# Splitting attention's small solves into halves between large matmuls, and preparing their operands earlier on VectorE

## The reference, cut to what matters

```python
x = x + 0.5 * moe(layernorm(x))
x = x + attn(layernorm(x))
x = x + 0.5 * moe(layernorm(x))
...
# attention, per sequence and head (4 heads of 32), in 8 chunks of 32 tokens
attn = -einsum('bhncd,bhned->bhnce', kbc, kc) * strict_lower
for i in range(1, chunk):
    upd = einsum('...j,...ji->...i', attn[..., i, :], attn[..., :, :i])
    attn = attn.at[..., i, :i].add(upd)
attn = attn + eye(chunk)
u = attn @ vc          # the values solve
w = attn @ kbc         # the keys solve
# then a scan over the 8 chunks
ui = ui - wi @ S; oi = qi @ S + a_loc @ ui; S = S + ki^T ui
...
# a multiscale causal convolution of v over 31 lags, a small gating network,
# a softmax mixture of the three branches, an RMS norm and an output projection
```

## Time and profile before

| | us |
|---|---|
| median of 3 runs | 1126.39 |
| lowest and highest run | 1124.57 and 1128.73 |
| the profiled execution | 1120.73 |
| its span, first to last instruction | 1118.9 |
| TensorE busy | 854.6 (76% of the span) |
| VectorE, ScalarE, GpSimd busy | 543.9, 335.9, 465.5 |
| mean granted TensorE clock | 0.898 |

### The profile page before, as it was taken

How to read it: one execution, slowest core, us unless ns; L and a number is a source line. 1 busy time by engine, 2 the same in 40 slices (tenths; PEclk the granted TensorE clock), 3 DMA queues, 4 the chain that set the end, 5 groups by cost and what they waited for, 6 DMA issues and landing times. The chain is left out here.

```text
span 1118.9 us, 26929 instructions
## 1 busy us (share of the span) xinstructions
PE 854.6 (76%) x11563; PEld 751.8 (67%) x11563; DVE 543.9 (49%) x1569; ACT 335.9 (30%) x646; POOL 465.5 (42%) x588
## 2 busy tenths in 40 slices
PE   4419999969558579988998899797526999799800
PEld 3419999969546457776777678665415999799800
DVE  6715565625455024575566356622623555445333
ACT  2214444324122112342234325311413444334200
POOL 1664479842233820870185028302024420323076
PEclk9999999979868869999999999986656999989955
DMA  7333434523100000000000000000004434334113
GB/s 266 131 109 112 142 116 125 157 88 94 56 26 2 0 22 4 2 20 32 4 2 21 4 4 1 21 4 21 1 17 139 133 125 136 107 118 143 55 40 110
DMA packets 68467, 75.71 MB, mean 68 GB/s; under 512 B 8150, under 2 KB 55165, under 8 KB 67836
## 3 DMA queue, kind: packets, MB, share of 16 engines
q1 hardware_dynamic: 60156, 57.27, 16.2%
q0 software_dynamic: 8192, 16.73, 4.7%
HBM read 47.82 MB, written 26.22 MB: 66 GB/s over the span
## 5 line engine op out<-in xcount | busy, mean ns | idle before, releaser
L237 POOL DMA_INDIRECT queue<-xn,slot x128 | 128.2, 1002 | 247.8 <-DVE slot L1459 104.7
L638 DVE TENSOR_TENSOR e_hid<-e_sg,e_pu 128x320 f32<-128x320 f32 x256 | 123.9, 486 | 195.8 <-ACT e_sg L594 134.1
L594 ACT ACTIVATE e_sg<-e_pg 128x320 f32<-128x320 f32 x256 | 111.6, 438 | 233.1 <-PE e_pg L556 162.4
L554 PE MATMUL e_pg<-e_xlo,e_whi 128*128 128x320 f32 x256 | 97.7, 382 | 23.6 <-issue 15.3
L243 POOL DMA_INDIRECT xn<-rows,slot x64 | 61.6, 963 | 123.2 <-ACT e_xhi L580 61.1
L684 POOL TENSOR_TENSOR a_prod<-a_inv,a_nmat 128x31 f32<-128x31 f32 (+15 forms) x124 | 64.5, 521 | 95.4 <-DVE a_nmat L1317 86.0
L541 PE MATMUL e_po<-expert,e_hid 128*128 128x128 f32 x640 | 86.2, 278 | 0.3 <-issue 0.3
L541 PE MATMUL e_po<-e_expert,e_hid 128*128 128x128 f32 x640 | 84.0, 276 | 1.3 <-DVE e_hid L638 1.3
L895 PE MATMUL a_pz<-a_vhi,lag_hi 128*128 128x512 f32 x184 | 79.3, 431 | 5.0 <-DVE a_vlo L1272 5.0
L541 PEld LDWEIGHTS e_po<-expert,e_hid 128*128 128x128 f32 x640 | 82.2, 194 | 0.5 <-issue 0.5
L541 PEld LDWEIGHTS e_po<-e_expert,e_hid 128*128 128x128 f32 x640 | 80.3, 193 | 1.8 <-DVE e_hid L638 1.8
(11 more groups left out here) (285 smaller groups left out, 1840.2 us busy)
## 6 DMA issues: line engine op xcount, KB each, us to landing
e_xs<-queue SPq DMA_DIRECT2D x32, 320.0 KB
rows<-e_rows SPq DMA_DIRECT2D x32, 320.0 KB, 2.7
expert<-wexp_in SPq DMA_DIRECT2D x14, 512.0 KB
e_expert<-wexp_in SPq DMA_DIRECT2D x14, 512.0 KB
queue<-r_zero SPq DMA_DIRECT2D x4, 1280.0 KB
expert<-wexp_in SPq DMA_DIRECT2D x14, 256.0 KB, 2.7
e_expert<-wexp_in SPq DMA_DIRECT2D x14, 256.0 KB
queue<-xn,slot POOLq DMA_INDIRECT x128
```

Of the source, the lines that this page charges most:

```text
L237: pool.indirect_dma_start(io.queue[c], bass.IndirectOffsetOnAxis(ap=k.slot[:, j, c:c + 1], axis=0), k.xn[:, j, :], None, bounds_check=SLOT ...
L554: pe.matmul(out, whi[par][:, i, fs], xlo[par][:, cols], start=True, stop=False)
L594: act.activation(sg[n % 2][:], pg[n % 2][:, 0:HALF], ACT.Silu).then_inc(silued, 1)
L638: dve.tensor_tensor(hid[q % 2][:, f, c * HALF:c * HALF + HALF], sg[n % 2][:], pu[n % 2][:, 0:HALF], ALU.mult).then_inc(hidden, 1)
```

## The change

Both solves take a range of chunks (`first`, `end`): the wait is only ahead of the first part, and the semaphore rises only after the last. In the front the second halves are cut in two: values in slots 1 and 2, keys in slots 3 and 4. In the tail of a stage that has both a group here and one ahead (g = 0, 1, 2), the first half of the next group's values stands in two parts between the last lag matmuls, and the keys stand in two parts on both sides of `channels(2a)`; `turn_mixture(2g+1)` and `output(2g+1)` then end the stage side by side. On VectorE `prepare(a)` moves from behind `rescale(2g+1)` to ahead of `mixture(2g+1)`. The stage of g = -1 keeps its order.

```diff
-            def solve_values(g, half):
-                if half:
+            def solve_values(g, half, first=0, end=HCH):
+                if half and not first:
                     pe.wait_ge(ukept, 2 * g + 1)
-                else:
+                elif not first:
...
-                for i in range(HCH):
+                for i in range(first, end):
...
-                mm.then_inc(usolved, 1)
+                if end == HCH:
+                    mm.then_inc(usolved, 1)
...
-                    if here and f == 1:
-                        solve_values(g, 1)
-                    if here and f == 3:
-                        solve_keys(g, 1)
+                    if here and f in (1, 2):
+                        solve_values(g, 1, 2 * (f - 1), 2 * f)
+                    if here and f in (3, 4):
+                        solve_keys(g, 1, 2 * (f - 3), 2 * (f - 2))
...
                 part = filler(9)
                 if here:
                     output(2 * g)
+                part = filler(6)
+                if here and ahead:
+                    solve_values(a, 0, 0, 2)
+                part = filler(6)
+                if here and ahead:
+                    solve_values(a, 0, 2, 4)
                 part = filler(SCALES)
+                if here and ahead:
+                    solve_keys(a, 0, 0, 2)
                 if ahead:
                     channels(2 * a)
+                if here and ahead:
+                    solve_keys(a, 0, 2, 4)
                 if g + 2 < NGRP:
                     turn(g + 2)
                 if here:
                     turn_mixture(2 * g + 1)
-                if ahead:
+                    output(2 * g + 1)
+                elif ahead:
                     solve_values(a, 0)
-                if here:
-                    output(2 * g + 1)
-                if ahead:
                     solve_keys(a, 0)
...
                 if here:
                     rescale(2 * g)
+                if ahead and here:
+                    prepare(a)
+                if here:
                     mixture(2 * g + 1)
...
-                if ahead:
+                if ahead and not here:
                     prepare(a)
```

More of the change, by code:

```diff
@@ L953, in solve_values, with solve_keys @@
                                            vh[strip(h), n, s, :], start=True, stop=True)
-                mm.then_inc(usolved, 1)
-            def solve_keys(g, half):
-                if half:
+                if end == HCH:
+                    mm.then_inc(usolved, 1)
+            def solve_keys(g, half, first=0, end=HCH):
+                if half and not first:
                     pe.wait_ge(wkept, 2 * g + 1)
-                else:
+                elif not first:
                     pe.wait_ge(weighted, g + 1)
                     behind(pe, crossed, 2 * g)
-                for i in range(HCH):
+                for i in range(first, end):
                     n = half * HCH + i
@@ L968, in solve_keys @@
                                            solve_w[strip(h), n * SEQS + s, :], start=True, stop=True)
-                mm.then_inc(wsolved, 1)
+                if end == HCH:
+                    mm.then_inc(wsolved, 1)
             def read(g, n):
```

## The result

| | before | after |
|---|---|---|
| median of the runs, us | 1126.18 (1124.57 to 1128.73, 4 runs) | 1141.18 (1134.64 to 1144.34, 4 runs) |
| ratio | | 1.0124, 95% interval 1.0075 to 1.0172 |
| profiled execution: time, span, mean granted clock | 1120.73, 1118.9, 0.898 | 1134.64, 1132.8, 0.889 |

I had forecast 1121.2 us with a range of 1116 to 1136. The time is 20 us above the forecast and outside the range. What happened has the shape and the higher price of my first rival: small matmuls went out in small pieces while GpSimd transferred.

A forecast was written before the change was run, and what follows sets the result against it. TensorE's order of work bounds stages 0 to 2, so only its idle gaps can give time. Tails 1.5 plus fronts 0.5, 1.1, 0.3 and 1.8 make 5.2 us; 1126.4 less this is 1121.2 us, range 1116 to 1136.

The forecast's parts named there:

- rival 1: Tail halves starve for code during GpSimd's transfers: 1131.3 us, or 1138 if not even the first half passes; chance 0.33.
- the tail's "is the operand there?": Stage 1's tail: operand ready at 602.0, so the first values half runs without a wait, 2 us to spare.
- if the stock carries the first half: Tails of stages 0 to 2: code stock lasts for the first values half, not the second; 10.1 us lost, 1131.3.
- The large matmuls ran at full speed there: Stages 0 to 2, during GpSimd's transfers: taken as a sign of some stock of code, perhaps enough.
- 17 us for the creep (5.4, 5.7, 5.8): Tails of stages 0 to 2: loss if not even the first values half gets through; less 5.2 gives 1138.
- the forecast's tails (22.33, 22.34, 21.03): Tails of stages 0 to 2, up to slot 1: together 1.5 us gained, nearly all of it in stage 0.
- The second output's wait: End of the tail: `output(2g+1)` loses its cover and waits nearly 1 us for ScalarE's copy.
- The rows' wait: Slot 1's wait for normalised rows grows to about 2 us (stages 1, 2) and 3.7 us (3).
- the gain of 2.1: Stage 0's tail: slot 1 at 513.1 against 515.22, with the 1.5 us gap and `channels`' 2.1 us wait before.
- the grid of 256: TensorE's issue gaps lie every 256 instructions, read as the next piece of code not being there yet.
- rival 2: Gaps belong to small matmuls, not the grid, so splitting removes none: about +3.4 us, 1129.8; chance 0.07.
- Stage 3: Stage 3's front: gaps of 0.6 and 1.33 us, no projections to wait for; gain 1.8 us, bounds 0 and 2.3.

The follow-up runs named there:

- experiment 13: Whole change without GpSimd's scatters in the tails of stages 1 and 2, against the kernel before at 1121 us: ratio 1.0024.
- experiment 2: Kernel before with only the tail's new order and the moved `prepare`, fronts as before, at the 1072 us level: ratio 1.0030.
- experiment 3: Changed kernel without GpSimd's scatters in the tails of stages 1 and 2, against the kernel before at 1072.12 us: 1070.79 us, ratio 0.9985.
- experiment 9: Changed kernel without GpSimd's scatters in the tails of stages 1 and 2, run again, against the kernel before at 1071 us: ratio 0.9994.
- experiment 10: Whole change, scatters of the tails of stages 1 and 2 issued one stage later, one at a time; against the kernel before at 1071 us: ratio 1.0014.
- experiment 4: Kernel before without GpSimd's scatters in the tails of stages 1 and 2, against the kernel before at 1072.12 us: 1070.77 us, ratio 0.9981.
- The front alone: Kernel before with only the fronts' second halves split, tail and `prepare` as before, at the 1072 us level: ratio 0.9981.

## Why the prediction was wrong, step by step

**The failed step is the tail's "is the operand there?".** I worked out when the operand is ready and let the values halves run at 0.65 + 0.09 us each from 603.9 and 606.1, inside transfers that the earlier trace rows date to 608.22: the slowing of small matmuls beside transfers stood at nothing in the sum. I named this in rival 1, and gave it 0.33 and a switch: "if the stock carries the first half". It did not, in any stage: 39 to 41 of its 64 pairs went through, and the rest crept, 5.1 us in stage 1. The earlier trace rows had two bursts inside a run of transfers and both crept; I had no row of a small burst that got through one. "The large matmuls ran at full speed there" was no evidence for the small ones: large ones use 128 instructions in 15 us, a values half uses 128 in 0.65. With no case of survival against two of creeping, the rival should have been the forecast.

**Its price was sound, its reason was not borne out.** I had 17 us for the creep (5.4, 5.7, 5.8), made up of the time to 1.4 us behind the last transfer. The price needs only that time, from the earlier trace rows, and not the supply of code that I named as the reason: no code was on its way while TensorE crept in stages 1 and 2. Measured against the forecast's tails (22.33, 22.34, 21.03) the change lost 6.3, 6.8 and 7.4, 20.6 us. Stage 1 splits into 5.1 for the creep and 1.8 for the clock, which I had left out. 1138 was named for this case, 1141.2 came.

**The lengths of the rest of the tail were right, and can be read in experiment 13.** Slot 1 of stage 1: forecast 22.34 us after `turn_mixture(2g)`, measured 22.29; stage 2: 21.03 and 21.31. `prepare` directly behind the first `rescale`: in VectorE's timeline of the changed kernel,

```profile
599.01 0.69 DVE L1426 TENSOR_TENSOR a_delta<-a_delta,a_ors 128x512 f32<-128x512 f32 x1
599.62 2.03 DVE L1335 STREAM_TRANSPOSE a_low<-a_inv 128x1024 f32<-128x1024 f32 x1
```

`channels` without a wait: yes. The second output's wait: 0.79 for "nearly 1". The rows' wait: 1.88 and 3.94 for "about 2" and 3.7. Stage 0's tail could not be seen free of creep at the higher level, since its gathers stayed in every run. At the lower level, without creep, it took 22.29 to 23.29 us (experiments 2, 3, 9 and 10) where I had 22.33; but experiment 4, with the old tail, took 22.02 there, so the gain of 2.1 was not to be had: the wait ahead of `channels` is 0.68 us in its stage 0 and not 2.12. So the creep is not the whole of the miss. Where nothing creeps the change stands level with the kernel before (experiments 3 and 4, and 1.0014 in experiment 10), and the forecast's 5.2 us do not appear.

**The fronts were half right.** No "issue" gap is left in the changed kernel's fronts of stages 0 to 2, which speaks for the grid of 256, as the times of the code's transfers do, and against rival 2. `silu_keys` makes TensorE wait 1.25 us where I had 1.75. The gain in time is smaller than the gaps that went (1.6 us of them in stage 1): stretches 0.7, 0.3 and 0.6 us shorter where I had 1.1, 0.3 and 1.8, and nothing in stage 0 (0.5). The front alone gave 0.9981, 2.0 us of 1072, with an interval of 0.2 to 3.9; my 3.7 is at its edge. Stage 3 is the term that was mis-sized; what hides there is not settled.

**The chances.** Slower had 0.23. Half of rival 1's weight sat on a price that needed the first half to get through, and that half had nothing behind it. The range ended at 1136, below the 1138 of the rival's other half, though that half alone had a sixth of the chances.

## What to carry over

Before you move a burst of small matmuls, look at what GpSimd's queue does at the new place: a run of indirect transfers can make TensorE creep through small matmuls, and large ones beside it show nothing of this. Where such transfers are not urgent, issue them one at a time between other work; here that turned a loss of 1.2 to 1.7% into a gain of 0.3% at the higher level (in different groups, each against its own kernel before), and brought nothing at the lower one. And lay the transfers of the instruction queue beside a gap before you put it down to code. If the trace shows two cases of a mechanism and none against it, it is the forecast and not the rival.

## What the runs showed of the hardware

- TensorE during a run of indirect transfers, at the higher level: 39 to 47 small pairs at full speed, then mostly 3 to 6 for each piece, a piece every 0.74 or 1.47 us, and full speed again 1.0 to 1.6 us after the last transfer. No piece of code moved in the creeps of stages 1 and 2; the means stays open.
- TensorE went on 1.3 to 1.6 us after a piece of its code had moved, at the four gaps named behind experiment 13. The Trainium skill (Runtime: NRT & Kernel Launch, "Instruction fetch mechanics") says that crossing a block of code is mostly hidden. The large matmuls of these traces agree (0.24 us apart where a piece of code moves, as at 624.13 in the changed kernel); the bursts of small ones don't (1.06 us at 614.05).
- The same program had two levels, 1071 to 1072 and 1120 to 1126 us, fixed within a group of runs. At the lower one the creep is missing with the same transfers beside it. Of the 48 us, 25 lie ahead of the first `turn_mixture(2g)` (490.8 in the kernel before, 466.0 in experiment 4), so the expert layer before attention has its share. What sets the level stays open: no run here varied it.
- The granted clock fell to its lower level, for 6.8 us, after TensorE had crept for 1.9, 2.9 and 3.5 us (stages 0, 1 and 2 of the changed kernel). After a full stop of 1.9 us it fell in some stages, for 3.4 us, and not in others.
